# The order around the first two head products: low heads, chunk 1, residual 1 and the gelu table in other places

## The reference

```python
# block 1 (L0)
y = layernorm(x) * (1 + gamma1(cond)) + beta1(cond)
x = x + attention(y) * alpha1(cond)          # 16 heads, softmax over 64 keys
z = layernorm(x) * (1 + gamma2(cond)) + beta2(cond)
x = x + (gelu(z @ fc1_w + fc1_b) @ fc2_w + fc2_b) * alpha2(cond)
# block 2 (L1)
h = layernorm(x) * (1 + scale(cond)) + shift(cond)
q, k = rotary(h @ wq + bq), rotary(h @ wk + bk)
x = x + softmax(q @ k.T / 4, masked) @ (h @ wv + bv) @ wo + bo
h = layernorm(x) * (1 + scale2(cond)) + shift2(cond)
x = x + gelu(h @ ff_w1 + ff_b1) @ ff_w2 + ff_b2
```

## Time and profile before

| | |
|---|---|
| median of 3 runs | 1885.76 us (1884.67 to 1885.84) |
| profiled execution, its own time | 1885.72 us |
| its span | 1883.9 us |
| TensorE busy | 1788.1 us, 95% |
| ScalarE busy | 1306.7 us, 69% |
| VectorE busy | 1237.4 us, 66% |
| GpSimd busy | 849.4 us, 45% |
| ACT_TABLE_LOAD | 93 at the gelu, 92 at the exponential, 1283 ns each |
| granted TensorE clock, mean | 0.986 of full speed |

### The profile page before, as it was taken

One profiled execution on the slowest core, in us unless ns is written; L12 is line 12 of the kernel. 1 busy time (PEld: TensorE's weight loads), 2 busy tenths in 40 slices (PEclk: granted clock), 3 DMA queues, 4 the chain that ended last, 5 costly groups with the idle time before them and its releaser, 6 DMA issues.

```text
span 1883.9 us, 41740 instructions
## 1 busy us (share of the span) xinstructions
PE 1788.1 (95%) x12623; PEld 1637.1 (87%) x12623; DVE 1237.4 (66%) x2985; ACT 1306.7 (69%) x2327; POOL 849.4 (45%) x1036
## 2 busy tenths in 40 slices
PE   4779999999999999999899999999999999999998
PEld 3668888888988888988889999999999999999986
DVE  4756667667667667666867667667667766666751
ACT  4337777777776776776668776776776677777663
POOL 2123333333333343333456655555665555566534
PEclk8889999999999999999999999999999999999999
DMA  6463435454434444344454233334323333333320
GB/s 166 107 147 95 100 97 133 117 128 111 97 96 119 122 122 122 89 105 108 124 149 109 84 108 98 98 107 114 84 86 105 101 103 106 103 84 97 93 71 34
DMA packets 330276, 199.84 MB, mean 106 GB/s; under 512 B 160995, under 2 KB 314597, under 8 KB 330213
## 3 DMA queue, kind: packets, MB, share of 16 engines
q1 hardware_dynamic: 330212, 199.06, 40.0%
HBM read 80.98 MB, written 17.33 MB: 52 GB/s over the span
## 4 chain that ended last, share of the span: by engine, by line
PE 73%; DVE 12%; issue 8%; SPq 2%; ACT 2%; DMA 1%; POOL 1%; DVEq 0%; POOLq 0%; ACTq 0%
PE D L1106 17%; PE C L912 16%; PE B L912 9%; PE B L1064 9%; PE A L1031 7%; PE B L1050 5%; PE A L912 5%; PE E L912 4%; DVE mx L1373 2%; SPq L329 2%; DVE o_sb L1397 2%; PE A L1036 2%; DVE exps L1379 1%; DVE ot_lo L1406 1%; PE E L1075 1%
## 5 line engine op out<-in xcount | busy, mean ns | idle before, releaser
L559 POOL TENSOR_TENSOR h_lo<-hact,h_hi 128x512 fp32r<-128x512 f32 x256 | 330.4, 1291 | 302.6 <-ACT h_hi L762 289.5
L1031 PE MATMUL A<-k_pad,q_pad 128*128 128x256 f32 x1536 | 259.9, 296 | 14.3 <-DVE exps L1379 9.3
L1106 PE MATMUL D<-wgt_hi,h_hi 128*128 128x256 f32 x1024 | 263.4, 290 | 0.0
L771 ACT COPY probs_turned<-B 128x512 f32<-128x512 f32 x256 | 147.7, 584 | 157.7 <-PE B L1050 157.7
L1064 PE MATMUL B<-v_blocks,probs_turned 128*128 128x68 f32 x2048 | 255.8, 272 | 0.4 <-ACT probs_turned L771 0.4
L1106 PE MATMUL D<-wgt_lo,h_hi 128*128 128x256 f32 x1024 | 255.7, 282 | 0.0
L1064 PEld LDWEIGHTS B<-v_blocks,probs_turned 128*128 128x128 f32 x2048 | 250.3, 193 | 5.8 <-ACT probs_turned L771 2.5
L757 ACT ACTIVATE hact<-C,b_col 128x512 f32<-128x512 f32 x256 | 176.1, 688 | 96.0 <-PE C L912 92.1
L1031 PEld LDWEIGHTS A<-k_pad,q_pad 128*128 128x128 f32 x1536 | 214.8, 194 | 18.3 <-issue 9.5
L1373 DVE TENSOR_REDUCE mx<-A 128x8 f32<-128x512 f32 x256 | 174.3, 681 | 69.3 <-PE A L1036 39.4
L766 ACT ACTIVATE exps<-exps 128x512 f32<-128x512 f32 x256 | 160.9, 630 | 76.3 <-DVE exps L1379 75.7
(11 more groups left out here) (140 smaller groups left out, 3944.0 us busy)
## 6 DMA issues: line engine op xcount, KB each, us to landing
k_pad<-k_flat SPq DMA_DIRECT2D x512, 64.0 KB, 2.1
q_pad<-q_flat SPq DMA_DIRECT2D x256, 128.0 KB, 2.3
gates<-gates SPq DMA_DIRECT2D x64, 256.0 KB, 4.5
x_bias<-x_bias SPq DMA_DIRECT2D x32, 512.0 KB, 3.5
rotation<-rotation SPq DMA_DIRECT2D x256, 64.0 KB, 1.9
x_in<-in_x SPq DMA_DIRECT2D x16, 512.0 KB, 4.2
gates<-gated_bias SPq DMA_DIRECT2D x32, 256.0 KB, 5.0
x_res<-in_x SPq DMA_DIRECT2D x16, 512.0 KB, 4.4
```

The lines of the kernel that those rows point to most:

```text
L559: pool.tensor_tensor(hb[1][:, m % 2, :], hact[:, m % 2, :], hb[0][:, m % 2, :].bitcast(F32), ALU.subtract).then_inc(h_lo, 1)
L1031: ins = nc.tensor.matmul(dst, qpad[g % 2][:, c, p, b, :, :].rearrange("p x s -> p (x s)"), kpad[g % 2][:, c, q, :, b * S:(b + 1) * S], sta ...
L1106: ins = nc.tensor.matmul(Dk[g // 2][:, (g % 2) * D:(g % 2 + 1) * D], hb[p][:, m % 2, g * P:(g + 1) * P], w_slice(q, W_FF2, D, m, 0, D), st ...
```

## The change

No arithmetic is added but one activation of one column whose result nobody reads; all else is the order of calls.

- TensorE: behind product 0 (`project(u, 0)`) come chunk 1 of the hidden layer and the turn of group 1's heads, and only then the two turns of y; `back` of chunk 0 comes ahead of product 1.
- VectorE: `low_heads` 0 goes ahead of the two maxima of group 2, which move behind it and behind residual 0; `low_heads` 1 ahead of subtract 1 of group 2 and of y's scale; residual 1, its statistics and its aggregate go behind both `y_low`, and in block 1 the gate of group 1 between these two.
- ScalarE: a one-column Gelu (`gelu_table`) stands behind the high heads of group 0, so that the table is loaded there; `hidden_high` of chunk 0 goes ahead of the high heads of group 1; the second exponential of group 2 ahead of the norm of group 1. Ahead of the first norm a wait for the three instructions of GpSimd that make `ident` and `minus_half` is added.

```diff
--- before.py
+++ after.py
@@ -146,6 +146,7 @@
         rs2 = sb("rs2", [P, G])
         nb2 = sb("nb2", [P, G])
         minus_half = sb("minus_half", [P, G])
+        table_probe = sb("table_probe", [P, 1])
         rtab = sb("rtab", [P, 2, S])
         mrow = sb("mrow", [P, TILE], F32R)
         mean_w = sb("mean_w", [P, P], F32R)
@@ -675,6 +676,7 @@
                     nc.scalar.copy(wgt[0][:, W_AT[n]], w_source(n, layer)).then_inc(w_hi[n], 1)
 
             def begin():
+                act.wait_ge(sem_ident, 3)
                 first_norm(0)
                 act.wait_ge(mod_done, 8)
                 first_columns(0, 0)
@@ -751,6 +753,10 @@
                         dst, src = value_views(pair, b, h)
                         nc.scalar.copy(dst, src).then_inc(v_moved, 1)
 
+            def gelu_table():
+
+                nc.scalar.activation(table_probe[:, :], minus_half[:, 0:1], ACT.Gelu)
+
             def hidden(tile, layer, m):
                 act.wait_ge(pe_f1, upto(tile, MC, m + 1))
                 await_(act, h_lo, upto(tile, MC, m - 1))
@@ -806,14 +812,16 @@
                 if b is not None:
                     move_probs(u, 1, 1)
                     high_heads(u, b, 0)
+                if c is not None:
+                    gelu_table()
                 if known(u) and u == NT + 1:
                     high_piece(3, 1, 3)
                 if c is not None:
                     hidden(u - 1, c, 0)
+                if c is not None:
+                    hidden_high(u - 1, 0)
                 if b is not None:
                     high_heads(u, b, 1)
-                if c is not None:
-                    hidden_high(u - 1, 0)
                 if c is not None:
                     hidden(u - 1, c, 1)
                     hidden_high(u - 1, 1)
@@ -827,8 +835,8 @@
                     hidden(u - 1, c, 2)
                 if b is not None:
                     exponential(u, 2, 0)
+                    exponential(u, 2, 1)
                     second_norm(u, 1)
-                    exponential(u, 2, 1)
                 if c is not None:
                     hidden_high(u - 1, 2)
                 if a == 0:
@@ -1141,17 +1149,18 @@
                     hidden(u - 1, 0)
                 if b is not None:
                     project(u, 0)
+                if c is not None:
+                    hidden(u - 1, 1)
+                if b is not None:
+                    turn_heads(u, 1, c)
                 if a is not None:
                     first_turn(u + 1, 0, b)
                     first_turn(u + 1, 1, b)
-                if b is not None:
-                    turn_heads(u, 1, c)
-                if c is not None:
-                    hidden(u - 1, 1)
+                if c is not None:
+                    back(u - 1, 0)
                 if b is not None:
                     project(u, 1)
                 if c is not None:
-                    back(u - 1, 0)
                     hidden(u - 1, 2)
                     back(u - 1, 1)
                 if a is not None:
@@ -1488,40 +1497,37 @@
                     output(u - 2, p, 1)
                 if b is not None:
                     reciprocals(u, 1, 0)
-                    maximum(u, 2, 0)
                     normalise_heads(u, 1, 0)
-                    maximum(u, 2, 1)
                     low_heads(u, b, 0)
                     reciprocals(u, 1, 1)
-                    subtract(u, 2, 0)
+                    maximum(u, 2, 0)
                     normalise_heads(u, 1, 1)
                 if b == 0:
                     gate_heads(u, 0)
                 if b is not None:
                     residual(u, b, 0)
+                    subtract(u, 2, 0)
+                    maximum(u, 2, 1)
+                    second_statistics(u, 0)
+                if b is not None:
+                    low_heads(u, b, 1)
                     subtract(u, 2, 1)
-                    second_statistics(u, 0)
                 if a is not None:
                     y_scale(u + 1, 0)
                 if b is not None:
                     second_aggregate(u, 0)
-                    low_heads(u, b, 1)
                 if a is not None:
                     y_shift(u + 1, 0)
                     y_scale(u + 1, 1)
+                    y_shift(u + 1, 1)
+                    y_low(u + 1, 0)
                 if b == 0:
                     gate_heads(u, 1)
                 if a is not None:
-                    y_shift(u + 1, 1)
+                    y_low(u + 1, 1)
                 if b is not None:
                     residual(u, b, 1)
-                if a is not None:
-                    y_low(u + 1, 0)
-                if b is not None:
                     second_statistics(u, 1)
-                if a is not None:
-                    y_low(u + 1, 1)
-                if b is not None:
                     second_aggregate(u, 1)
                 if known(u) and u == NT + 1:
                     low_piece(2, 1, 3)
```

## The result

The changed kernel took 1891.94 us (1891.32 to 1894.97, six runs) where the kernel before took 1885.80 (1884.59 to 1886.65, six runs beside them): a ratio of 1.0038, 95% interval 1.0027 to 1.0050. The change makes the kernel 6.1 us slower, and the interval leaves out 1. The forecast was 1887.6, range 1876 to 1897, with the larger chance (0.38) on a time that cannot be told from no change and 0.36 on a slower one. Span of the profiled execution: 1890.3 us against 1883.9, 6.4 more.

What follows compares the result with a forecast made beforehand. TensorE, busy 95%, sets the time, but ScalarE's full row was taken to hold what follows; block 1 -4.1, block 2 +7.8 and ends -1.9 sum to +1.8 on 1885.76: 1887.6 us, range 1876 to 1897.

Steps and rivals of the forecast that it cites:

- Block 1, -0.27 a step: Middle steps of block 1: ScalarE 0.16 us earlier plus 0.11 slack lets TensorE gain 0.27 a step, -4.1 us.
- the new wait: Middle step of block 1: TensorE comes early and waits some 0.8 us for probs_turned of group 2.
- Block 2, +0.52 a step: Block 2: first copy of group 2 1.46 later, less slack 0.94, delays TensorE's weighing by 0.52 a step, +7.8 us.
- The table: ScalarE's gelu table load and one-column activation, taken as 0.2 us, lie in ScalarE's idle time and cost nothing.
- Rival D: ScalarE's table load holds longer than its row, gelu up to 0.9 later: 27 us at most, 1914; chance 0.02.
- h_lo of chunk 1, 0.3 inside the back product: TensorE's back product: a wait of 0.3 for h_lo 1, named among the places waits might merely move to.
- The ends, -1.9: First step -0.7, step between the blocks -0.7, last step -0.5: together -1.9 us, bounds -4 and +1.
- The first step: Very first step, no hidden layer beside it: queries wait for y_lo, now ahead of residual 1 and statistics: -0.7.
- A: Waits go, the norm of group 1 does not pace in block 2: -10 us, 1876; chance 0.26.
- B: The chain to ScalarE's norm of group 1 is 0.3 longer in both blocks: +11 us, 1897; chance 0.24.
- Its sign for block 2: ScalarE's norm of group 1 starting later than 1269.4 in block 2 decides for the slower rival.
- C: Both blocks and ends: waits are only moved and cancel, the change does nothing: 1885.8; chance 0.08.

Runs made afterwards that it cites:

- norm_late: The changed kernel with ScalarE's norm of group 1 moved behind the high part of chunk 3: 1867.65 us, 0.9905 to the kernel before.
- low_first: norm_late with GpSimd's low part of chunk 1 ahead of group 0's rs and nb, ScalarE's high part of y 1 ahead of group 0's norm: 1858.78 us.
- low1_back: residual_back with VectorE's low heads of group 1 put back behind y's scale 0 and aggregate 0: 1865.36 us, 0.9892 to the kernel before.
- residual_back: The changed kernel with VectorE's y, gate 1 and residual 1 in the order of before: 1874.13 us, 0.9932 to the kernel before.
- low_first_residual: low_first with residual 1, statistics, aggregate and gate of group 1 put back among the y pieces: 1864.42 us, 0.9886 to the kernel before.
- chunk_table: The kernel before with chunk 1 between the products, ScalarE's hidden_high 0 moved ahead and the early gelu table, VectorE as before: 1874.33 us, 0.9941.

## Why the prediction was right, and where its sizes were off

**Block 1, -0.27 a step: right.** Measured -0.25; over its 14 steps that are not at an end, -3.9 us (forecast -4.1). The first of the 14 gave 0.45, at a granted clock of 0.93 of full speed instead of 0.88, so a part of that is luck. The gelu came at 801.86 in before's times (801.88 forecast), chunk 1 at 802.61 (802.62), shift 1 at 808.34 (808.36), the aggregate at 811.77 (811.73), the norm at 813.74 (813.70), the keys' high part at 814.76 (814.71), the new wait at 0.81 (0.8).

**Block 2, +0.52 a step: right in its mechanism, too small.** Measured +0.75, and +10.2 us over the block's 14 steps from the step of +0.75 behind the boundary to the one of +0.43, where the forecast had +7.8. The mis-sized term is this +0.52 x 15. Its dates held within 0.07: norm 1270.00 (forecast 1269.94), copy 1273.01 (1272.94). But the sum took the late start of the weighing for the whole price. It came 0.61 late instead of 0.52 (the copy 0.07 later than forecast, the matmul 0.02 more behind it), and its 16 matmuls took 1.78 from start to start instead of 1.70, and a further 0.07 fell behind it at chunk 7: 0.61 + 0.08 + 0.07 = 0.76. So of what the sum lacked a step, 0.09 lay in the start and 0.15 behind it. The sum followed low heads 1 as it stood, so its chain has the delay of that call in it, though its words name only the turn and the residual.

**The table: right.** In both blocks load and one-column activation lie in time that ScalarE sat idle, and no drain shows: the activation starts 1.29 behind the load's start. Its 0.20 is the value taken. Rival D is out, and with it the 1.38 that the Trainium skill (ScalarE: Activation LUTs, What ACT_TABLE_LOAD costs) adds to a load.

**h_lo of chunk 1, 0.3 inside the back product: seen, wrongly left out of the account.** It stands as idle time 0.21; from the last hi matmul ahead of it to the query product behind it pass 1.07 (1321.56 to 1322.63 in block 2), where the same stretch of chunk 0's back product takes 0.60, so 0.47 in all. TensorE comes to the weighing before the copy even so, so it should cost nothing in this kernel; no run takes it alone out of the changed kernel. norm_late shows it as the next in line, low_first and low1_back take it away and return 0.48 and 0.50 a step in block 2, against norm_late and residual_back.

**The ends, -1.9: wrong, +0.1 measured.** The steps between the blocks and the last one gave -1.4 (forecast -1.2): -0.35 and -0.70 at the boundary, -0.33 at the end. The first step was to gain 0.7 and lost 1.5. Its waits before, TensorE:

```profile
64.60 0.47 PE L912 MATMUL E<-wgt_hi,ot_hi 128*128 128x256 f32 x2 [1.29 <-DVE ot_lo L1406]
...
68.79 0.47 PE L912 MATMUL E<-wgt_hi,ot_hi 128*128 128x256 f32 x2 [1.75 <-DVE ot_lo L1406]
...
71.88 1.19 PE L912 MATMUL A<-y_hi,wgt_hi 128*128 128x512 f32 x2 [2.14 <-DVE y_lo L1320]
```

And in the changed kernel:

```profile
66.82 0.44 PE L1083 MATMUL E<-ident,o_sb 128*128 128x128 f32 x2 [1.05 <-DVE x_res L1431]
...
68.95 0.48 PE L920 MATMUL E<-wgt_hi,ot_hi 128*128 128x256 f32 x2 [0.38 <-DVE ot_lo L1415]
...
72.81 1.22 PE L920 MATMUL A<-y_hi,wgt_hi 128*128 128x512 f32 x2 [2.91 <-ACT y_hi L724]
```

From the weighing before these (62.29 before, 63.21 after) to the queries it is 9.59 and 9.60: residual and statistics no longer stand ahead of y_lo, but y itself is turned only behind residual 0 and subtract 0, so the 0.7 never came. The loss of 1.5 lies on both sides of this stretch, 0.9 ahead of the weighing and 0.6 behind the first queries. Ahead of it, from 50 to 60 us, the granted clock was 0.83 of full speed in the profile of before and 0.59 here, with TensorE busy 7.2 of 10 us in both; the first queries run at the lower level in both (1.2 GHz of 2.4), 1.19 and 1.22 for two matmuls that take 0.63 in the middle steps. The 0.9 is not the change's doing: six of the runs above execute the changed code up to this weighing and have it between 61.77 (norm_late) and 62.61 (low_first_residual), around the 62.29 of before. The clock in that stretch does not explain it alone either: it was 0.69 in norm_late and 0.83 in low_first_residual. How much of the 0.6 behind the queries the change brings about stays open: no run separates it.

The steps add up to -3.9 + 10.2 + 0.1 = +6.4, and the span is 6.4 longer. Against the forecast of +1.8 the miss is made of +2.4 in block 2, +2.0 at the ends and +0.2 in block 1; no two of them cancel.

**Rivals.** A (nothing paces in block 2) is out: the norm of group 1 started at 1270.00, and A's bound was 0.5 earlier than the sum. B had the right side and place, and its +0.82 a step in block 2 is nearer to the measured 0.75 than the forecast's 0.52. But its price came from a chain 0.3 longer, where it was 0.04 and 0.06 longer; the rest of the way towards B lay between the copy and the matmuls, and in these. Its sign for block 2, a norm later than 1269.4, could not tell it from the forecast, whose own sum had 1269.94. C is out by the interval.

What the forecast did not ask is whether the parts need each other. chunk_table shows that the order of TensorE and the table alone gain 11 us, and the changed kernel that VectorE's edits (with the norm behind both exponentials) turn this into a loss of 6. Most of that hung on one call, the norm of group 1, whose place nothing required; with it moved, low heads 1 ahead of aggregate 0 is what still costs block 2, by way of h_lo.

## What to carry to other kernels

When an operand is made later on one engine, look for the consumer's place in the next engine's list, and whether anyone waits for that consumer soon: here a norm nobody needed yet blocked ScalarE's row, and moving it behind that row was worth 24 us. A wait that is taken away passes on to the next operand that was just in time, also in a part where nothing waited before; so list the slack of each operand behind the edit, not only the one it frees. And price the parts of a change one by one as well as together, since delays that each fit in the slack may not fit in it at once.

## What was not expected of the hardware

A wait of TensorE costs more than its idle time. The weighing without a wait takes 1.90 as a group, with one 1.97 to 2.08; from start to start of what follows it lost 0.08, the last third of a back product 0.09 (0.57 instead of 0.48). With two waits a step that is an estimated 2.5 us a block of 15 steps, and the longer groups show in the page as busy time. Part of the 2.08 of block 1 may be a wait inside the group instead: its last eight matmuls need ScalarE's second copy, which ends at 817.24, about where they are due.
